# Block searches as sums of signs on ScalarE, and the first block's keys ahead of four attribute one-hots, in a five-layer GIN kernel

## The reference

```python
def _gin_conv(x, src, dst, edge_attr, w1, b1, bn_w, bn_b, w2, b2, ew, eb):
    edge_emb = edge_attr @ ew.T + eb
    n = x.shape[0]
    agg_x = jax.ops.segment_sum(x[src], dst, num_segments=n) + x
    agg_e = jax.ops.segment_sum(edge_emb, dst, num_segments=n) + eb
    h = jnp.concatenate([agg_x, agg_e], axis=1)
    h = h @ w1.T + b1
    mean = jnp.mean(h, axis=0)
    var = jnp.mean((h - mean) ** 2, axis=0)
    h = (h - mean) * jax.lax.rsqrt(var + BN_EPS) * bn_w + bn_b
    h = jax.nn.relu(h)
    return h @ w2.T + b2
...
h = jnp.maximum(_layernorm(x, axis=-1), 0.0)
# five _gin_conv layers, a relu between them
x = x + _L0_gnn_ref(h, edge_attr_16, ...)
```

## Time and profile before

| what | value |
|---|---|
| time, median of 3 runs | 654.82 us (654.66 to 655.7) |
| the profiled execution | 658.63 us |
| its span | 656.8 us |
| PE busy | 613.7 us (93%) |
| DVE busy | 331.2 us (50%) |
| ACT busy | 261.0 us (40%) |
| mean granted clock of TensorE | 0.983 |

### The profile page before, as it was taken

How to read it: one execution, slowest core, us unless ns; L and a number is a source line. 1 busy time by engine, 2 the same in 40 slices (tenths; PEclk the granted TensorE clock), 3 DMA queues, 4 the chain that set the end, 5 groups by cost and what they waited for, 6 DMA issues and landing times.

```text
span 656.8 us, 12887 instructions
## 1 busy us (share of the span) xinstructions
PE 613.7 (93%) x5447; PEld 373.6 (57%) x5447; DVE 331.2 (50%) x663; ACT 261.0 (40%) x569; POOL 72.4 (11%) x90
## 2 busy tenths in 40 slices
PE   6788898978999989999999999999999999999996
PEld 6676787745555544844446644447544457444456
DVE  6799999979999928522113421125311216101034
ACT  0268977755677715601115411117211128012133
POOL 5550135510221100000000000000000000000000
PEclk9899999998999999999999999999999999999999
DMA  5981001000000000000000100000100000100033
GB/s 143 318 277 11 2 4 27 6 4 5 4 3 4 4 5 1 26 9 1 1 1 1 33 1 1 1 1 1 33 1 1 1 1 2 31 2 1 1 96 102
DMA packets 13320, 19.22 MB, mean 29 GB/s; under 512 B 2263, under 2 KB 7397, under 8 KB 13251
## 3 DMA queue, kind: packets, MB, share of 16 engines
q1 hardware_dynamic: 12099, 16.00, 8.1%
q0 software_dynamic: 1152, 2.20, 1.4%
HBM read 16.26 MB, written 1.60 MB: 27 GB/s over the span
## 4 chain that ended last, share of the span: by engine, by line
PE 59%; DVE 2%; ACT 1%; issue 0%; POOLq 0%; DVEq 0%
PE bank L1338 39%; PE bank L1402 9%; PE bank L1374 8%; PE bank L1368 2%; ACT h L1458 1%; DVE bn_stats L1562 1%; DVE h L1583 0%; DVE h L1584 0%; PE bank L1385 0%; PE bank L252 0%; DVE h L1603 0%; ACT bn_small L1471 0%; PE bank L1327 0%; DVE bn_small L1578 0%; DVE bn_small L1577 0%
## 5 line engine op out<-in xcount | busy, mean ns | idle before, releaser
L1338 PE MATMUL bank<-adj,h_pieces 128*128 128x504 bf16 (+1 forms) x1372 | 263.5, 351 | 0.0
L1338 PEld LDWEIGHTS bank<-adj,h_pieces 128*128 128x128 f16 x1372 | 123.0, 97 | 141.4 <-issue 10.2
L1562 DVE BATCH_NORM_STATS2 bn_stats<-bank 128x6 f32<-128x504 f32 (+1 forms) x70 | 42.8, 627 | 219.3 <-PE bank L1374 218.7
L971 ACT ACTIVATE adj<-bank 128x450 bf16<-128x450 f32 x175 | 95.3, 547 | 65.3 <-PE bank L829 60.0
L1449 ACT ACTIVATE aggT<-bank 128x504 f32<-128x504 f32 x24 | 14.2, 590 | 261.0 <-PE bank L1374 223.7
L444 DVE TENSOR_TENSOR h<-iota_lo,h 128x1536 bf16<-128x1536 bf16 (+2 forms) x95 | 87.5, 921 | 8.2 <-PE bank L829 7.1
L853 PE MATMUL bank<-h,adj 128*17 128x40 f32 (+11 forms) x1752 | 79.3, 206 | 11.2 <-DVE h L639 6.2
L829 PE MATMUL bank<-h 128*128 128x75 bf16 x1064 | 69.3, 201 | 17.5 <-DVE h L444 16.1
L453 PE MATMUL bank<-adj,h_pieces 128*128 128x450 bf16 x343 | 83.6, 356 | 1.6 <-issue 1.6
L829 PEld LDWEIGHTS bank<-h 128*128 128x128 bf16 x1064 | 54.9, 100 | 49.8 <-DVE h L444 30.0
L853 PEld LDWEIGHTS bank<-h,adj 128*17 128x17 f32 x1752 | 69.2, 104 | 18.1 <-DVE h L639 10.5
(11 more groups left out here) (151 smaller groups left out, 364.5 us busy)
## 6 DMA issues: line engine op xcount, KB each, us to landing
adj<-attr SPq DMA_DIRECT2D x1, 2524.5 KB
adj<-attr SPq DMA_DIRECT2D x1, 1963.5 KB
weights<-wpack SPq DMA_DIRECT2D x5, 323.0 KB
out<-h SPq DMA_DIRECT2D x6, 256.0 KB
adj<-attr SPq DMA_DIRECT2D x1, 1402.5 KB
adj<-attr SPq DMA_DIRECT2D x2, 561.0 KB
h<-mpack SPq DMA_DIRECT2D x5, 179.0 KB
adj<-order SPq DMA_DIRECT2D x2, 202.0 KB, 2.9
```

Of the source, the lines that this page charges most:

```text
L971: nc.scalar.activation(out_view(u), bank_view(n % CNT_BANKS), ACT.Copy).then_inc(s_ev, 1)
L1338: last = nc.tensor.matmul(agg_ps[b][:, 0:w], hp[:, k, s, :], adj[:, k, c * LW:c * LW + w], start=(k == 0 and s == 0), stop=stop and s == p ...
L1562: V.bn_stats(stats[:, h, ds(c * 6, 6)], w1_ps[b][h][:, 0:cols]).then_inc(st_last if last and h == 1 else st_done, 1)
```

## The change

Two things are changed. ACT takes over the searches of blocks 1 to 8: with the threshold 2t-1 in `odd_thr`, `Sign(-2v + 2t - 1)` is 1 for each value v below t and -1 for the others, so the sum over n values is twice the count less n. The eight row searches run on ACT ahead of its first key copies; the search within block 1's row comes behind these copies, and those of blocks 2 to 8 behind ACT's copies of strips 7 to 13. DVE keeps block 0's searches and a short instruction or two for each result: `row_indices_of_signs` makes the row's number and 256 times it, `block_starts_of_signs` adds the sum within the row. Block 1's start and the row numbers of blocks 2 to 8 are now made in strip 0. POOL has two more short iotas, and the same order of gathers.

And block 0's keys are made on DVE behind the attribute one-hots 0 to 3, ahead of 4 and 5; PE transposes them behind attribute steps 0 to 3.

```diff
@@ DVE's helpers
+                    def row_indices_of_signs(a, b):
+
+                        dve.wait_ge(s_less, b - 1)
+                        steps.then(V.tensor_scalar(row_i[0:GB, a:b], sign1[0:GB, a:b], 0.5, 0.5 * FIRSTS, ALU.mult, ALU.add))
+                        V.tensor_scalar(row_base[0:GB, a:b], row_i[0:GB, a:b], float(WIN), 0.5 * WIN, ALU.mult,
+                                        ALU.add).then_inc(s_lidx, 1)
+
+                    def block_starts_of_signs(b):
+
+                        dve.wait_ge(s_within, b)
+                        V.scalar_tensor_tensor(start_i[0:GB, b:b + 1], sign2[0:GB, b:b + 1], 0.5, row_base[0:GB, b:b + 1],
+                                               ALU.mult, ALU.add).then_inc(s_start, 1)
@@ DVE's program
                     steps.then(rows_before(0))
                     row_indices(0, 1)
-                    steps.then(rows_before(1))
-                    row_indices(1, 2)
+                    row_indices_of_signs(1, 2)
...
                     dst_one_hots(0)
                     dst_one_hots(1)
                     block_starts(0)
-                    block_starts(1)
-                    for i in range(2, LEAD):
+                    dst_one_hots(2)
+                    dst_one_hots(3)
+                    keys(0)
+                    for i in range(4, LEAD):
                         dst_one_hots(i)
-                        rows_before(i)
-                    keys(0)
-                    for b in range(LEAD, BLOCKS):
-                        last = rows_before(b)
-                    steps.then(last)
-                    row_indices(2, BLOCKS)
...
                         if u == 0:
+                            block_starts_of_signs(1)
+                            row_indices_of_signs(2, BLOCKS)
                             dve.wait_ge(l_c, 16)
...
                             if u == starts_strip(b):
-                                block_starts(b)
+                                block_starts_of_signs(b)
@@ PE's program
                     for i in range(LEAD):
+                        if i == 4:
+                            transposes(0)
                         attr_step(i)
-                    transposes(0)
@@ ACT's program
+                    def row_signs(b):
+
+                        n = in_block(b)
+                        nc.scalar.activation(less_st(b), first_i[0:n, :], ACT.Sign, scale=-2.0, bias=odd_thr[0:n, b:b + 1],
+                                             accum_out=sign1[0:n, b:b + 1]).then_inc(s_less, 1)
+
+                    def within_signs(b):
+
+                        n = in_block(b)
+                        act.wait_ge(s_row[b], 16)
+                        nc.scalar.activation(within_st(b), row_st(b), ACT.Sign, scale=-2.0, bias=odd_thr[0:n, b:b + 1],
+                                             accum_out=sign2[0:n, b:b + 1]).then_inc(s_within, 1)
+                    act.wait_ge(s_first, 16)
+                    act.wait_ge(s_thr, 2)
+                    for b in range(1, BLOCKS):
+                        row_signs(b)
                     keys_out(0)
+                    act.wait_ge(s_less, BLOCKS - 1)
+                    within_signs(1)
...
                         nc.scalar.activation(out_view(u), bank_view(n % CNT_BANKS), ACT.Copy).then_inc(s_ev, 1)
+                        for b in range(2, BLOCKS):
+                            if u == starts_strip(b) - 1:
+                                within_signs(b)
```

More of the change, by code:

```diff
@@ L380, in gin_program @@
             s_thr = sem("thresholds_made")
+            s_less = sem("firsts_signs_summed")
+            s_within = sem("in_row_signs_summed")
             s_lidx = sem("row_indices_made")
@@ L533, in _ @@
                                    allow_small_or_imprecise_dtypes=True).then_inc(s_thr, 1)
+                    nc.gpsimd.iota(odd_thr[:, 0:1], [[0, 1]], base=-1, channel_multiplier=2 * GW,
+                                   allow_small_or_imprecise_dtypes=True)
+                    nc.gpsimd.iota(odd_thr[:, 1:BLOCKS], [[2 * GW * GB, BLOCKS - 1]], base=2 * GW * BLOCK0 - 1,
+                                   channel_multiplier=2 * GW, allow_small_or_imprecise_dtypes=True)
                     nc.gpsimd.iota(thr[:, BLOCKS:BLOCKS + 1], [[0, 1]], base=0, channel_multiplier=CW,
```

4 lines of the change are left out of this document (added).

## The result

| kernel | median of 5 runs | from, to | profiled execution | its span |
|---|---|---|---|---|
| before | 655.45 us | 654.66 to 656.62 | 658.63 us | 656.8 us |
| changed | 659.80 us | 657.60 to 660.63 | 659.54 us | 657.8 us |

The ratio of changed to before is 1.006, with an interval from 1.0043 to 1.0078. The change costs 4.3 us. The forecast was 654.5 with a range of 651.8 to 657.0, and a chance of 0.50 that the difference would be within 0.2%.

The account below looks back on a forecast made before the run. DVE was taken to set the pace up to about strip 70, PE close behind. 1.8 us gained, 3.5 lost at the keys, 2.2 returned, 0.2 lost to ACT: 0.3 gained, 654.82 to 654.5 us, range 651.8 to 657.0.

Parts of the forecast that it names:

- The first one-hots at 16.35 us: DVE's first counting one-hots, before at 18.12 us, come at 16.35 without its row searches: 1.8 us gained.
- Block 1's keys at 26.0 after 3.9 us of waiting: Pair gather 1, issued at 18.7, takes 7.3 us; DVE waits 3.9 and starts these keys 1.7 later than before.
- The stretch to strip 8: From block 1's keys to strip 8, 2.9 us of waits for PE run beside the 3.9: 34.4 instead of 34.93.
- returned by the stall: Term of the sum between block 1's keys and strip 8: 2.2 us returned by the stall that runs beside.
- Every sign that the prediction named as its proof: In the changed profile: one-hots at 16.4, DVE idle 3 to 5 us before keys at about 26, ACT gapless strips 7 to 14.
- Half clock behind the wait: After PE's longer idle time ahead of block 1's keys, half clock costs 0 to 1.5 us, taken as 0.7.
- Strips 7 to 14 at ACT's pace: ACT needs 12.1 us instead of 11.75 from its copy of strip 7 to that of 14; 0.3 us remain gained.
- Behind strip 14 all is constant: Behind strip 14 neither DVE nor PE has less or other work; later gathers, overflow step and SP are unchanged.
- The wait and the stall add up: Rival: keys at 26.5, PE's late matmuls come behind the wait, DVE 2.2 us late at strip 8: 657.1 us, chance 0.16.
- The gather that lands soon: Rival: pair gather 1 takes 3.1 us, block 1's keys start at 22.1, 2 us gained in the end: 652.6, chance 0.16.
- the slow search on ACT: Rival: a search costs 0.75 us instead of 0.49, ACT needs 1.8 more for strips 7 to 13: 656.3, chance 0.06.

Follow-up runs that it names:

- again_before: The kernel before, unchanged, timed and profiled a second time: 655.70 us, ratio to before 0.9994.
- start1_early: Changed kernel with block 1's search ahead of ACT's first key copies and its start ahead of block 0's keys: 653.74 us, ratio to before 0.9966.
- keys1_strip7: Changed kernel with block 1's keys made at strip 7 instead of 3, its start and pair gather still late: 655.80 us, ratio to before 0.9995.
- start1_early_2: start1_early repeated unchanged in another set: 653.79 us, ratio to before 0.9973.
- again_after: The changed kernel, unchanged, timed and profiled a second time: 658.67 us, ratio to before 1.0049.
- warm_waits: Changed kernel with 26, 24 and 10 useless matmuls filling PE's idle time around the transposes of blocks 0 and 1: 661.00 us, ratio to before 1.0082.
- start1_early_keys_late: start1_early with block 0's keys behind all six attribute one-hots and its transposes behind all six steps: 662.40 us, ratio to before 1.0054.
- start1_early_late_loads: start1_early with SP's last attribute and weight loads held until block 8's row gather has landed: 653.63 us, ratio to before 0.9972.
- start1_strip2: Changed kernel with block 1's start made in strip 2 instead of strip 0: 664.29 us, ratio to before 1.0077.

## Why the prediction was wrong, step by step

- **The first one-hots at 16.35 us.** Right: 16.02. ACT's row searches lie beside other work at a spacing of 0.61 to 0.63 us, 0.61 forecast.
- **Block 1's keys at 26.0 after 3.9 us of waiting.** Right: 25.31 after 3.35, 26.20 after 3.25 and 26.69 after 4.92 in three profiles. The issue was at 18.40, forecast 18.7, and it was read 6.9 us later, forecast 7.3. The latency was taken from thinner rows than the text says: the landings in the earlier trace rows are of four gathers issued from 23.58 to 27.85 us, and the one of 18.51 has none on record. The other profiles bear it out: issued at 11.80 in again_before this gather took 2.9 us, at 13.40 in start1_early 6.0, at 18.2 to 18.6 in the changed kernel's profiles and keys1_strip7 6.9 to 8.4. The Trainium skill, "DMA: Bandwidth & Descriptors", section "Anatomy of one DMA — SWDGE (gpsimd) path", led to 2.3 us and no wait. The measurement decides against it here: 6.9 us, and 3.9 for row gathers of the same size with the loads held back.
- **The stretch to strip 8, "these waits run beside the 3.9 us and need not be paid twice".** This is the step that failed. In absolute time it was good: the forecast put ACT's copies of strips 7 and 14 at about 34.8 and 46.9, and they started at 34.88 and 47.08. That is partly luck, since the keys started 0.7 us earlier than forecast and the way from them to strip 7 took 9.6 us in place of 8.8. What was wrong is the 2.2 us "returned by the stall": 2.9 us of waits for PE were read out of one execution of before as if they were part of the kernel, and again_before has only 0.71 and 0.19 us of waits for PE from 23 to 34 us. There was nothing to run beside. Set against again_before, the terms of the sum are 2.4 us gained (forecast 1.8), 3.2 lost at the keys (3.5), 1.7 lost from there to strip 7 (2.2 returned) and 0.9 lost to ACT (0.2): 3.35 lost at strip 14 in place of 0.3 gained. The third term is off by 3.9 us, and the errors of the others nearly cancel. Every sign that the prediction named as its proof appeared, because all of them look at the changed kernel and none at whether the kernel before usually has that stall. The profile's page gave the hint itself: 658.63 us was 3.8 us above the median of 654.82 known then, outside the runs' whole range to 655.7, and I carried a difference over to the median without asking where those 3.8 us lay.
- **Half clock behind the wait, 0 to 1.5 us, taken as 0.7.** Not separated: strips 4 to 7 took 0.8 to 1.7 us more than without the wait, in three profiles of the changed kernel with 6.54, 7.07 and 6.12 against 5.35 us (again_before 5.07, start1_early_2 5.67), which includes whatever else is late there. And part of the half clock only moved: from 20 to 26 us the clock was 0.72 in again_before and 0.99 in the changed kernel.
- **Strips 7 to 14 at ACT's pace, 12.1 us.** Right: 12.20, 12.21 and 12.22 in three profiles. The search of 256 columns is spaced 0.49, and DVE's four waits for it add up to 4.1 us. Its price was set against 11.75, of the first profile; against again_before's 11.33 it is 0.9 instead of 0.35. That what is lost there stays lost isn't borne out in full: in both pairs of profiles the kernels are even by strip 20, by 0.5 us of catching up and 0.7 of a pause of PE.
- **Behind strip 14 all is constant.** Mostly: again_after is 4.8 us behind again_before at strip 14 and 4.0 at strip 76 and in the span. The profile in the result is 3.35 behind at strip 14, 0.7 at strip 20, where again_before has a stall of PE of its own, 1.0 at strip 76, and 2.9 in the span; 1.8 of it were added between 148 and 168 us, where the granted clock is 0.57 from 148 to 156 against 0.84 there in again_before.
- **The rivals.** "The wait and the stall add up" gave 657.1 with 0.16, and has the right sign and about the right place, the keys at 26.5. But its mechanism isn't what happened: the stall wasn't paid behind the wait, it wasn't there in either. The loss is the wait, which puts the keys 0.8 to 2.2 us behind again_before's, and what comes behind it up to strip 7, in which the clock has a share; ACT's pace shows in the profiles up to strip 14 and gave nothing back when it was undone. The gather that lands soon and the slow search on ACT didn't happen.

**What stays open**: why PE stalls for issue in some executions and on one chip more than on others; why the searches on DVE cost 1 to 2 us; and why warm_waits was slower than the changed kernel. The exact share of the half clock wasn't isolated either.

## What to carry to other kernels

If the profiled execution is slower than the whole range of the timed runs, find out where before using any wait in it: a stall with no releaser on record may belong to that execution alone, and nothing may be counted as hidden beside it until a second profile shows it too. When searches or other short work move to another engine, keep the issue of the first gather that depends on them where it was, since its latency under the bulk loads was 7 us and not 3. An engine that newly sets the pace for a few strips may cost less in the end than it does there; look some strips further before pricing it, and look at the engine behind the copies too.

## What was not expected of the hardware

- PE can stand still with nothing that it waits for on record ("issue"), 0.3 to 1.7 us at a time. With a DMA share of 1.05 to 1.06 from 20 to 40 us it did so not at all in again_before's stretch to 36 us, for 1.62 and 0.95 us in keys1_strip7, and eight times for about 0.45 in start1_early_keys_late. Full DMA queues aren't needed for it. again_before has one at a later place, which strip 20 feels, and there the DMA share (the last column but one of the second row) is 0.00; that of start1_early_late_loads at 57.85 came with 0.00 from 57 to 58 us too:

```profile
54.46 0.66 PE L853 MATMUL bank<-h,adj 128*17 128x40 f32 x14 [1.66 <-issue]
```

```profile
52.00:54.00 2.00, 0.80 (x16) 0.63 (x16) 0.88 (x2) 0.77 (x5) 0.00 (x0) 1.00 0.00 0
```

- PE was idle for 2.60 us ahead of 26.32 and for 1.03 ahead of 27.74, and from 26.0 to 32.6 us the granted clock was 0.50, although PE was busy for 5.25 us of it. With 24 and 10 other matmuls put into these idle times, which left 1.76 and 0.57 us of them, the clock still fell, but later, and the stretch had 0.74. From 15.6 to 19.0 us, behind its 26 extra matmuls, warm_waits had 1.00 where the changed kernel had 0.50, but start1_strip2 had 1.00 there without them, so that isn't shown to be their doing.
